# All fetches of the sparse experts issued ahead of all scatters, with a slot for every expert

## The reference

```
E, G, TOPK, HID, INTER, A_INTER = 32, 16, 2, 128, 256, 128
cap = int(1.25 * T / E)                                   # 80 tokens an expert
probs = softmax(gelu([xf, stats(xf)] @ r1_w.T + r1_b) @ r2_w.T)
topp, topi = top_k(probs, 2);  wnorm = topp / topp.sum()
idx = argsort(-score, axis=0)[:cap].T                     # each expert's 80 tokens
w = Wc.T[idx] * valid                                     # weight of each chosen token
xe = xf[idx]                                              # gather
gate, upv = split(einsum('eci,eji->ecj', xe, w_up))
ye = einsum('ecj,eoj->eco', silu(gate) * upv, w_down)
out = zeros((T, C)).at[idx].add(w[..., None] * ye)        # scatter
# and 16 adapters, one for every two experts, on the tokens that were kept
ah = silu(ag) * av;  out = out + einsum('tg,tgo->to', 0.05 * Wmask_by_group, ah @ a_down)
```

## Time and profile before

| | us |
|---|---|
| median of 3 runs | 1969.56 |
| lowest and highest of them | 1966.38 and 1974.54 |
| the profiled execution, its own time | 1975.11 |
| its span, first to last instruction | 1973.3 |
| mean granted TensorE clock in it | 0.889 |
| sparse experts in it, first fetch to the next stage | 1246.9 to 1371.3 |

### The profile page before, as it was taken

The page is one execution under the profiler, slowest core; times in us unless marked ns, Lnnn a source line. Parts: engine busy times, 40 slices in busy tenths (PEclk is TensorE's granted clock), DMA queues, the critical chain, the costliest instruction groups (busy, mean ns, idle before and its releaser), DMA issues. The chain is left out here.

```text
span 1973.3 us, 22476 instructions
## 1 busy us (share of the span) xinstructions
PE 1573.8 (80%) x7280; PEld 684.7 (35%) x7280; DVE 1037.0 (53%) x2148; ACT 931.0 (47%) x1573; POOL 409.9 (21%) x369
## 2 busy tenths in 40 slices
PE   4799997999658997668699870586599986699997
PEld 1344443334213332233234430484122223244443
DVE  8577771100028999645477529322678843433332
ACT  4766665322358886411266640122267773243333
POOL 4110100000058898200022200451111100100000
PEclk7799998999859999969899885686689996899999
DMA  5111201000000000000111081002212102000000
GB/s 135 45 43 38 58 18 60 0 0 0 23 4 5 4 3 3 28 1 0 34 38 28 30 327 35 14 18 77 74 58 66 59 8 101 5 1 0 0 0 21
DMA packets 51804, 72.16 MB, mean 37 GB/s; under 512 B 11281, under 2 KB 44329, under 8 KB 49942
## 3 DMA queue, kind: packets, MB, share of 16 engines
q1 hardware_dynamic: 49654, 69.16, 11.5%
q0 software_dynamic: 2048, 1.73, 0.4%
HBM read 48.26 MB, written 18.12 MB: 34 GB/s over the span
## 5 line engine op out<-in xcount | busy, mean ns | idle before, releaser
L656 ACT ACTIVATE a_probs_sb<-a_t_ps 128x512 f32<-128x512 f32 x512 | 286.8, 595 | 129.1 <-PE a_t_ps L537 72.7
L747 DVE CUSTOM_DVE_ANT_0 a_biased<-a_s_ps,a_bias 128x512 f32<-128x512 f32 x256 | 166.2, 686 | 67.8 <-issue 67.7
L533 PE MATMUL a_t_ps<-a_stack 126*128 126x512 bf16 (+1 forms) x512 | 169.5, 394 | 30.5 <-DMA a_stack<-a_least_parts 11.7
L514 PE MATMUL a_s_ps<-a_stack 96*128 96x512 bf16 (+1 forms) x512 | 155.3, 412 | 39.2 <-DMA a_stack<-a_stacks 25.0
L1429 DVE TENSOR_TENSOR_SCAN s_h<-s_dA,s_dbu 128x1024 f32<-128x1024 f32 x64 | 146.6, 2290 | 52.9 <-POOL s_dbu L1394 44.3
L754 DVE TENSOR_REDUCE a_least_sb<-a_s_ps 128x2 f32<-128x1024 f32 x128 | 152.6, 1221 | 34.6 <-PE a_s_ps L514 34.4
L1394 POOL TENSOR_TENSOR s_dbu<-s_du,s_bs 128x1024 f32<-128x1024 f32 x64 | 151.7, 2383 | 30.1 <-DVE s_h L1429 28.5
L2809 ACT ACTIVATE c_hid<-c_up_ps,c_b 128x512 f32<-128x512 f32 x128 | 88.0, 687 | 142.9 <-PE c_up_ps L2778 142.9
L2819 DVE TENSOR_TENSOR c_gated_sb<-c_hid,c_g_ps 128x2048 f32<-128x2048 f32 x32 | 73.2, 2288 | 145.8 <-ACT c_hid L2809 145.8
L552 PE MATMUL a_o_ps<-a_probs_sb,a_vpad 128*16 128x512 f32 x1024 | 138.7, 615 | 0.2 <-ACT a_probs_sb L656 0.2
L2778 PE MATMUL c_up_ps<-xT,c_w 128*128 x256 | 117.4, 602 | 5.9 <-DMA c_select<-in_c_select 5.9
(11 more groups left out here) (448 smaller groups left out, 2584.3 us busy)
## 6 DMA issues: line engine op xcount, KB each, us to landing
x_wu<-in_x_wu SPq DMA_DIRECT2D x2, 4096.0 KB, 17.8
a_stacks<-a_p SPq DMA_DIRECT2D x16, 384.0 KB, 3.1
a_stack<-a_stacks SPq DMA_DIRECT2D x32, 192.0 KB, 3.7
a_stack<-a_stacks SPq DMA_DIRECT2D x64, 96.0 KB, 2.3
a_stacks<-a_p SPq DMA_DIRECT2D x16, 256.0 KB, 2.4
q_q<-q_q SPq DMA_DIRECT2D x32, 128.0 KB, 2.3
x_wd<-in_x_wd SPq DMA_DIRECT2D x2, 2048.0 KB, 33.6
c_w<-in_c_w SPq DMA_DIRECT2D x2, 2048.0 KB, 10.2
```

The costliest lines, as they stand in the source:

```text
L514: made = nc.tensor.matmul(s_ps[:, 2 * (x % 2) + e, :], operand(0, k, pair, e, SCORE_ROWS)[:, t * P:(t + 1) * P], operand(1, k, pair, e, SC ...
L533: last = nc.tensor.matmul(out, operand(1, k, pair, e, TURNED_ROWS)[:, t * P:(t + 1) * P], operand(0, k, pair, e, TURNED_ROWS), start=True, ...
L656: nc.scalar.activation(probs[:, y % PROB_RING, e, :], bank("turned", y, e), ACT.Exp, scale=-1.0).then_inc(probs_ready, 1)
L747: nc.vector.tensor_tensor_reduce(out=biased[:, e, :], in0=s_ps[:, 2 * (x % 2) + e, :], in1=bias[:, h, at:at + N], scale=1.0, scalar=3.0e38 ...
```

## The change

`X_RING` is gone. `x_got` and `x_results_sb` have a slot for every expert (32 in place of 8). GpSimd issues the fetches of all 32 experts one after another, with no wait between them, and then all 32 scatters. Each fetch has a semaphore of its own (32 in place of 8), and all scatters count on one (1 in place of 8). ScalarE no longer waits for a scatter before it writes a result. `weigh` runs for 2 experts at a time in place of 4, so 16 times in place of 8, after the first expert of each pair.

```diff
-X_RING = 8
@@ sparse_experts
-    SOME = 2 * PAIR
+    SOME = PAIR
-    fetched = [core.flag(f"x_fetched{n}") for n in range(X_RING)]
-    scattered = [core.flag(f"x_scattered{n}") for n in range(X_RING)]
+    fetched = [core.flag(f"x_fetched{n}") for n in range(E)]
+    scattered = core.flag("x_scattered")
-        got = core.sb(mem, "x_got", [CAP, X_RING, X_ROW])
+        got = core.sb(mem, "x_got", [CAP, E, X_ROW])
-        results = core.sb(mem, "x_results_sb", [CAP, X_RING, C])
+        results = core.sb(mem, "x_results_sb", [CAP, E, C])
@@ sync
-            for n in range(X_RING):
-                sp.wait_ge(scattered[n], 16 * E // X_RING)
+            sp.wait_ge(scattered, 16 * E)
@@ gpsimd
             def fetch(e):
-                if e >= X_RING:
-                    pool.wait_ge(turned, (e - X_RING) // PAIR + 1)
-                    pool.wait_ge(weighed, (e - X_RING) // SOME + 1)
                 nc.gpsimd.indirect_dma_start(
-                    out=got[:, e % X_RING, :], ...).then_inc(fetched[e % X_RING], 16)
+                    out=got[:, e, :], ...).then_inc(fetched[e], 16)
             def scatter(e):
                 pool.wait_ge(placed, e // SOME + 1)
                 pool.wait_ge(result_ready, e + 1)
-                nc.gpsimd.indirect_dma_start(... in_=results[:, e % X_RING, :] ...).then_inc(scattered[e % X_RING], 16)
+                nc.gpsimd.indirect_dma_start(... in_=results[:, e, :] ...).then_inc(scattered, 16)
-            for e in range(X_RING):
+            for e in range(E):
                 fetch(e)
             for e in range(E):
-                if e + X_RING < E:
-                    fetch(e + X_RING)
                 scatter(e)
@@ tensor, turn
-                    pe.wait_ge(fetched[e % X_RING], 16 * (e // X_RING + 1))
+                    pe.wait_ge(fetched[e], 16)
@@ scalar, result
-                if e >= X_RING:
-                    act.wait_ge(scattered[e % X_RING], 16 * (e // X_RING))
@@ vector, weigh
-                first = q * SOME % X_RING
-                for n in range(SOME):
-                    dve.wait_ge(fetched[first + n], 16 * (q * SOME // X_RING + 1))
-                rows = got[:, first:first + SOME, :]
+                for e in range(q * SOME, (q + 1) * SOME):
+                    dve.wait_ge(fetched[e], 16)
+                rows = got[:, mine, :]
```

More of the change, by code:

```diff
@@ L2301, in fetch @@
             def fetch(e):
-                if e >= X_RING:
-                    pool.wait_ge(turned, (e - X_RING) // PAIR + 1)
-                    pool.wait_ge(weighed, (e - X_RING) // SOME + 1)
                 nc.gpsimd.indirect_dma_start(
-                    out=got[:, e % X_RING, :], out_offset=None, in_=rows_dram,
-                    in_offset=bass.IndirectOffsetOnAxis(ap=fetch_at[:, e:e + 1], axis=0)) \
-                    .then_inc(fetched[e % X_RING], 16)
+                    out=got[:, e, :], out_offset=None, in_=rows_dram,
+                    in_offset=bass.IndirectOffsetOnAxis(ap=fetch_at[:, e:e + 1], axis=0)).then_inc(fetched[e], 16)
             def scatter(e):
@@ L2314, in scatter @@
                     out=results_dram, out_offset=bass.IndirectOffsetOnAxis(ap=put_at[:, e:e + 1], axis=0),
-                    in_=results[:, e % X_RING, :], in_offset=None, bounds_check=2 * T - 1,
-                    oob_is_err=False).then_inc(scattered[e % X_RING], 16)
+                    in_=results[:, e, :], in_offset=None, bounds_check=2 * T - 1,
+                    oob_is_err=False).then_inc(scattered, 16)
             pool.wait_ge(rows_stored, 16)
             pool.wait_ge(results_zeroed, 32)
-            for e in range(X_RING):
+            for e in range(E):
                 fetch(e)
             for e in range(E):
-                if e + X_RING < E:
-                    fetch(e + X_RING)
                 scatter(e)
@@ L2333, in turn @@
                     e = PAIR * g + n
-                    pe.wait_ge(fetched[e % X_RING], 16 * (e // X_RING + 1))
-                    last = nc.tensor.transpose(t_ps[g % 2][:, n * CAP:(n + 1) * CAP], got[:, e % X_RING, 0:C],
+                    pe.wait_ge(fetched[e], 16)
+                    last = nc.tensor.transpose(t_ps[g % 2][:, n * CAP:(n + 1) * CAP], got[:, e, 0:C],
                                                core.ident[0:CAP, 0:CAP])
@@ L2392, in result @@
                 act.wait_ge(weighed, e // SOME + 1)
-                if e >= X_RING:
-                    act.wait_ge(scattered[e % X_RING], 16 * (e // X_RING))
-                nc.scalar.activation(results[:, e % X_RING, :], d_ps[e % 2][0:CAP, 0:C], ACT.Copy,
+                nc.scalar.activation(results[:, e, :], d_ps[e % 2][0:CAP, 0:C], ACT.Copy,
                                      scale=weight[:, 0, e:e + 1]).then_inc(result_ready, 1)
```

## The result

The changed kernel takes 1973.14 us (median, 1969.23 to 1976.78), the kernel before 1967.69 us in the same session. The ratio is 1.0021, with a 95% interval of 1.0011 to 1.0031: 2 to 6 us slower. The profiled execution took 1971.87 us, with a span of 1970.1. That is less than the 1975.11 of the profiled execution before, so two single profiles can't show where those few us lie. Outside the stretch of the sparse experts, where nothing was changed, the profiles of this document differ by up to 18 us. So I compare that stretch alone in profiles, and whole times only by medians.

A forecast was written before the change was run, and what follows sets the result against it. It took the TensorE, ScalarE and VectorE loop with its holds as the bound, GpSimd nearly as long. Semaphores +1.2, first half +6 and second half -16 made -9 us on 1969.6: 1961 us, range 1946 to 1980.

The forecast's parts named there:

- Holds stay away under scatters alone: Sparse experts' second half: TensorE's late-result stalls vanish once GpSimd only scatters; last 8 pairs at 4.05 us each, -16 us.
- The first half, +6 us: Sparse experts until 1304: GpSimd occupied without a break, charged near one further hold; bounds 0 and 13.5 us.
- The slower rival: Sparse experts: an unbroken run of indirect DMAs holds TensorE more often, 15 us lost, 1986 us; chance 0.20.
- No effect: Sparse experts: TensorE's holds have another cause and go on under scatters alone; 1971 us; chance 0.32.
- GpSimd alone is left: Sparse experts: holds vanish in the first half too, GpSimd's 64 DMAs set the end; -27 us, 1943; chance 0.10.
- Semaphores, +1.2: Stage's end: GpSimd clears 17 more semaphores at 0.071 us each with nothing to hide it, +1.2 us.
- Weights by pairs, 0: VectorE: eight more `weigh` runs are covered by TensorE's other work, 0 us; at most 8.2 us if uncovered.
- Waits that went, 0: GpSimd's, ScalarE's and SyncE's waits that the change removes: 0 us on the path, GpSimd having 27 us of slack.
- Scatters in one go to 1304: GpSimd after the fetches: about nine results waiting at 1286, scattered every 1.24 us until the queue empties at 1304.

The follow-up runs named there:

- e6: Changed kernel with GpSimd's 32 fetches as plain transfers of neighbouring rows, gather left out: 1944.90 us, ratio 0.9871 to the kernel before.
- e7: Changed kernel with plain fetches by SyncE, gather left out, and 32 fills of 128 x 1024 on GpSimd ahead of its scatters: 1950.76 us, ratio 0.9911.
- e10: Changed kernel with a fill of 128 x 512 on GpSimd behind each fetch, fetches 1.73 us apart: 1974.58 us, ratio 1.0039.
- e1: Changed kernel with GpSimd's order undone: eight fetches, then fetch and scatter in turns as before: 1971.01 us, ratio 1.0001.
- e5: e2 plus 32 indirect fetches by GpSimd into a spare tile that nobody reads, ahead of its scatters: 1969.80 us, ratio 1.0009.
- e14: e5 with spare fetches of 16 rows in place of 80: 1972.01 us, ratio 1.0018.
- e2: Changed kernel with the 32 fetches issued by SyncE as plain transfers of neighbouring rows, gather left out: 1934.44 us, ratio 0.9830.
- e3: Changed kernel with weights made for four experts at a time, as before: 1972.07 us, ratio 1.0015.
- e12: Changed kernel with one semaphore per pair of fetches, fills behind 26 fetches (1.62 us apart) and the first 10 scatters: 1960.84 us, ratio 0.9947.
- e11: Changed kernel with a 128 x 128 fill on GpSimd behind each fetch and behind the first 14 scatters: 1972.55 us, ratio 1.0020.

## Why the prediction was wrong

The time fell within the range, and the direction was not the one forecast. That the time stayed so near the kernel before's is the luck of two changes of 16.7 us that cancelled.

*Holds stay away under scatters alone:* right. No hold from 1294.58 on; -16.7 us for the second half, -16 predicted. The reason given ("only scatters", 57% of the time occupied) was half right: it is their distance, 1.9 us on average, that keeps holds away. Scatters 1.22 apart hold as fetches do (e6, e7, e10).

*The first half, +6 us:* this is the step that failed. I charged one further hold, bounds 0 and 13.5; it was +16.7. I looked at the share of time in which GpSimd is occupied (76% to 100%), and priced the rest of the way at one more short hold. But GpSimd's being occupied costs 0.2 us a pair at most (e7; nothing in e10). In close order without a pause TensorE all but stops: one pair in 36.5 us. The first 8 fetches, which I named as the nearest row, ran while TensorE had only begun, and could not show it. There is a reason in the rows why no hold of before grew so long, though no run tests it alone: a scatter waits for a result, so a hold soon stops GpSimd as well, and with it the transfers that go with the hold (GpSimd waits 23.0 us for results, 10 times). The 24 fetches that were moved ahead wait for nothing. e1, which gives the turns of fetch and scatter back, has short holds again.

*The slower rival* (chance 0.20, 1986) had the loss of the first half nearly right, 15 us, by another way (pairs of 10.8 us each, where one took 36.5), and then assumed today's pace for the second half. Each case had one half right, and I never priced them together: 1.2 + 15 - 16 = 0, which is what happened.

*No effect* (0.32, 1971) gave the time nearly, for another reason: the holds did not go on as they were. With the rule of the Trainium skill (SBUF — State Buffer, SBUF: two separate sides) stood the conclusion that the order of GpSimd's DMAs is nothing to TensorE. e5 refutes that conclusion: 32 transfers that nobody reads cost 35 us. It does not show that the memory's sides contend: a fifth of the rows holds as long (e14), and SyncE's transfer of the same bytes holds nothing (e2). By the recorded starts it is TensorE's completions that are held, not its access; with modelled ends that is a reading and not shown. The Trainium skill (DMA: Bandwidth & Descriptors, SWDGE vs HWDGE vs iDMA) states that descriptors for GpSimd's transfers are made by software on GpSimd, and those for SyncE's by hardware. e2 and e5 fall on the two sides of that line; but e6, made by GpSimd too, held nothing until its scatters began, with 32 packets a transfer as in the changed kernel, so the software's descriptors as such are not enough.

*GpSimd alone is left* (0.10, 1943): GpSimd's sum was never the bound, because TensorE's loop all but stops beside transfers in close order. In the changed kernel the 106.05 us from the first fetch to the last scatter are 46.1 to the end of the hold, in which TensorE got through less than two pairs, 53.5 to the start of the last pair, and 6.4 behind it. That the kernel before comes to 106 as well, by many short holds, is not explained.

*Semaphores, +1.2:* right, 5.97 us for the gap. *Weights by pairs, 0:* nothing shows, within the interval (e3). *Waits that went, 0:* nothing shows either (e1 has them gone too). *Scatters in one go to 1304:* wrong; nine results were to be waiting when the fetches ended, and one was.

Of the 2 to 6 us by which it is slower, 1.2 are in the gap at the stage's end. The profiles show no more (+1.05 from first fetch to next stage), and the rest is not placed. What in the chip delays TensorE's completions is open too. One rival is left untested: every execution here was recorded with its span and clock, so the recording itself may have a part in the holds, and no unrecorded one was tried.

## What to carry to other kernels

Two engines that wait for nothing of each other can still slow each other. Look at what the one gets done in the stretch where the other is dense, before you move more work into that stretch: a reordering may only move the loss. To learn whether an engine waits for a transfer's data or for the transfer's being there, run it once more into a tile that nobody reads. A queue with slack can be too fast: with the new order, a fill of 0.4 us behind 26 of its transfers and a shorter one behind 10 (and 15 semaphores fewer than in the changed kernel) took 9 us off the kernel before, where the new order alone added 2 to 6.

## What the runs showed of the hardware

- Beside indirect transfers of GpSimd 1.15 to 1.22 us apart, over 32 of them, TensorE's completions nearly stop (a pair of 3.83 us takes 36 to 40). 1.41 apart they leave a quarter to a third of the pace (pairs of 11.1 to 14.3 us), 1.52 about half (5.4 to 10.2), 1.62 and 1.73 all of it (3.83). It sets in about 3 us after the first where TensorE is at full pace (e6, e7), some 8 us after it in e5 and 11 in the changed kernel, and clears 2 to 8 us after the last. All this was seen in recorded executions only.
- It goes by the instruction: 80 rows of 528 bytes, 80 of 512 and 16 of 528 hold alike (39.8, 39.6 and 38.3 us for the pair), and scatters 1.22 apart hold as gathers do (e6, e7, e10). Plain transfers by SyncE, or by GpSimd (0.52 us each, with as many packets), and fills do not.
- An indirect transfer of 80 rows occupies GpSimd 0.91 us and one of 16 rows 0.85, with 0.30 us to the next.
- Beside fills of 128 x 1024 on GpSimd, one pair took 3.84 us and four took 4.03 or 4.04, in place of 3.83.
- The gap at the stage's end grows with the semaphores, by 1.20 and 1.50 us for 17 more. Between two runs with fills, 16 more take it from 5.21 us (e12, 62 of them) to 6.33 (e11, 78), 0.07 us each; two kernels with 77 differ by 0.3 us for a reason that is not shown.
